# A three-part decoder block on one core: cross attention's scores in 32x128 tiles, low parts in strips, and a few new orders

## The chip, the core and the metric

The kernel runs on one core of one Trainium2 chip. The core has TensorE (PE; its loads of the stationary operand are PEld), VectorE (DVE), ScalarE (ACT), GpSimd (POOL) and the DMA queues that SyncE (SP) issues. The metric is the device time of one execution in microseconds (us), as the median of three. Where times are compared, only what differs by more than a fifth of a per cent is told apart.

## The reference

Everything is fp32, on 32 sequences of 64 tokens with 512 channels. Cut to what matters:

```python
def attn(x, wq, wk, wv, wo):              # 32 heads of 16, 8 key/value heads, causal
    scores = einsum('bihd,bjhd->bhij', q, k) * 16 ** -0.5
    return softmax(where(causal, scores, min)) @ v -> @ wo

def xattn(h, ctx, mask, Wq, Wk, Wv, Wo, q_norm_w, k_norm_w):   # 32 heads of 128, 8 key/value heads
    q = rmsnorm(h @ Wq.T) * q_norm_w
    k = rmsnorm(ctx @ Wk.T) * k_norm_w
    scores = einsum('bhqd,bhkd->bhqk', q, repeat(k, 4)) / sqrt(128) + mask
    return softmax(scores) @ repeat(v, 4) -> @ Wo.T

def ffn(h, ...):                          # shared expert and a latent path
    shared = (relu(h @ up_w) ** 2) @ down_w
    routed = ((h @ fc1_w) @ expert_w) * sum(top_2(h @ gate_w)) @ fc2_w
    return layernorm(shared + routed) * gamma + beta

x = x + attn(layernorm(x)); x = x + xattn(layernorm(x), ctx, mask); x = x + ffn(layernorm(x))
```

## The kernel before

The 32 sequences are worked in two halves of 16 (1024 tokens, 8 tiles of 128 tokens). Each half goes through three stages: self attention, cross attention, and the feed-forward part. The program of each engine is written out by hand as one list of instructions; semaphores (counts) tie the lists together, so the order in which a function calls its helpers is the order on that engine.

The large products are made of three fp32r products each (`split_mm`, L440): high by high, high by low, low by high, where the low part is what the rounding to fp32r left over. ACT makes the high part of a weight piece (`split_piece` of ACT, L938), POOL (L1836) or DVE (L1614) the low one. Weight pieces pass through a ring of three staging buffers (`stage`), and a load waits until the low part of the piece three before it is made.

**Projections of self attention** (`first_projections`, `second_projections`, L598 on for PE): keys/values `kv0` to `kv3`, queries `q0` to `q3`, transposes of normed tiles (`norms`) and of context tiles (`contexts`). `self_attention` (L633) then transposes the keys (`kt0`, `kt1`), makes `q4` and `q5`, and walks 16 sequences: step p makes the scores of sequence p+2, the transposes of the probabilities of p, the value products of p-1, and pieces of output projection. For every sequence DVE spreads the keys over eight groups (L1518), takes maxima and sums, POOL subtracts the maxima (L1866) and multiplies by the reciprocals (L1872), and ACT takes the exponentials. In steps 2, 4, 6 and 8 POOL also makes the low parts of the first four weight pieces of cross attention, two of 512 columns and two of 1024, each with one instruction (L1953).

**Cross attention** runs over 8 groups of heads (one key/value head, four query heads) and 4 chunks of 256 tokens: 32 slots a half, 64 in all. Of a slot, PE's part is `slot` (L791): output projection of chunk k, scores of chunk k+2 (`scores2`, L738), transposes of the probabilities of k+1 (L766), key/value projection of k+4, value product (L782), query projection of k+4. In `scores2` the 128 head channels are cut into four parts of 32 (j), as DVE's transposes leave them; the four 32-token blocks of queries lie in the four row groups of the array (i). The stationary operand of a matmul is 32 channels by 64 columns (two heads of 32 queries), the moving one 32 channels by 64 keys, and the output goes to half of the partitions of bank i of `quad`. So eight tiles of 32x64 of the array are in use in turn. The operands are plain fp32, for which the trace shows two records a matmul.

**Feed-forward** (`last_turn_and_ffn`, PE L805 on): for every chunk of 256 tokens `up` in four parts, `latent`, `down` for two tiles, and `transpose_latent`. The two banks `acc0` and `acc1` take turns in a fixed order (the tables FFN, BETWEEN and LAST), so a matmul group waits until the group two before it has been evacuated. DVE's `result` (L1692) takes the statistics of a finished tile, its normed value (L1706) and adds it to x (L1711, which also needs a value from POOL); `latent_lo` (L1686) evacuates the transposed latent.

Of the kernel before, what the change touches and what calls it, by code (L numbers as in the profile page):

```python
# [7 lines left out]
F32 = mybir.dt.float32  # L8
FR = mybir.dt.float32r
BF16 = mybir.dt.bfloat16  # L10
ALU = mybir.AluOpType
# [6 lines left out]
SEQ = 64  # L18
# [41 lines left out]
SELF_END = "kt0 kt1 q4 q5 q6 q7 lx0 lx1 lx2 lx3 lx4 ckv cq0 cq1"  # L60
# [3 lines left out]
BETWEEN = (FFN + " *ln0 *ln1 latt3 up30 up31 up32 up33 *ln2 *ln3 *ln4 *ln5 *ctx0 *ctx1 *ctx2 *ctx3 *ln6 *ln7 "  # L64
           "*ctx4 *ctx5 *ctx6 *ctx7 " + SELF_END)
# [8 lines left out]
def ffn_numbered(names):  # L74
# [5 lines left out]
        for names in ("kv0 kv1 q0 q1 kv2 q2 kv3 q3", "kv0 kv1 q0 kv2 q1 q2 kv3 q3")]  # L80
# [42 lines left out]
def decoder_block(nc, x_in, ctx_in, mask_in, w_self, w_cross, qn_in, kn_in, w_ffn,  # L123
                  f1g_in, expt_in, fc2_in, gamma_in, beta_in, out):
    with ExitStack() as stack:
# [313 lines left out]
        def _(pe):  # L439
# [177 lines left out]
            def second_projections():  # L617
                self_kv(1, 0)
                norms(1, 4)
                self_kv(1, 1)  # L620
                self_queries(1, 0)
                contexts(1, 0)
                self_kv(1, 2)
                contexts(1, 2)
                self_queries(1, 1)
                norms(1, 6)
                self_queries(1, 2)
                contexts(1, 4)
                self_kv(1, 3)
                contexts(1, 6)  # L630
                self_queries(1, 3)

            def self_attention(half):  # L633
                place = Place(1, half)
                at = place.at
                pe.wait_ge(proj_out.sem, at(proj_out, PROJ[half]["kv3"] + 1))
                for m in range(2):
# [44 lines left out]
                self_queries(half, 4)  # L682
                scores1(0)
# [121 lines left out]
            def last_turn_and_ffn(half):  # L805
# [102 lines left out]
                norm(6)  # L908
                down(0, 1)
                norm(7)  # L910
# [26 lines left out]
        def _(act):  # L937
# [110 lines left out]
            def second_projections():  # L1048
                place = Place(1, 1)
                norms_hi(1, 2)  # L1050
                act.wait_ge(acc_rdy.sem, Place(3, 0).at(acc_rdy, A3[0]["up32"] + 1))
                split_piece(place, 3)
                norms_hi(1, 4)
                self_kv(1, 0)
                self_kv(1, 1)

                act.wait_ge(x_out.sem, Place(3, 0).at(x_out, NT))
                self_queries(1, 0)
                contexts_hi(1, 0)
# [4 lines left out]
                self_queries(1, 1)  # L1064
                norms_hi(1, 6)
                self_queries(1, 2)
                contexts_hi(1, 4)
                split_piece(place, 5)
                self_kv(1, 3)
                contexts_hi(1, 6)  # L1070
                self_queries(1, 3)

            def self_attention(half):
                place = Place(1, half)
                at = place.at
                for m in range(2):
                    n = A1[half][f"kt{m}"]
                    act.wait_ge(acc_rdy.sem, at(acc_rdy, n + 1))
                    nc.scalar.copy(kt[:, m * COLS:(m + 1) * COLS], acc[n % 2][:]).then_inc(acc_free[n % 2].sem, 1)

# [23 lines left out]
                self_queries(half, 4)  # L1104
                def second_norm_hi(i):
                    n_at, n = lx(half, i)
                    transposed_hi(n_at, n, tile_of(xn_hi, i), ln_hi_done)

                for p in range(-AHEAD, NSEQ + 1):
# [23 lines left out]
                    if p in (2, 4, 6, 8):  # L1133

                        if p > 4:
                            act.wait_ge(acc_rdy.sem, at(acc_rdy, A1[half]["q7"] + 1))
                        else:
                            act.wait_ge(proj_rdy.sem, at(proj_rdy, PROJ[half]["kv3"] + 1))
                        split_piece(Place(2, half, 0), (p - 2) // 2)
# [180 lines left out]
        def _(dve):  # L1320
# [147 lines left out]
            def second_projections():  # L1468
                norms_lo(1, 4)
                contexts_lo(1, 0)  # L1470
                first_statistics(1, 6)
                first_statistics(1, 7)
                first_norm(1, 6)
                first_norm(1, 7)
                contexts_lo(1, 2)
                norms_lo(1, 6)
                contexts_lo(1, 4)
                contexts_lo(1, 6)
# [30 lines left out]
            def self_attention(half):  # L1509
                at = Place(1, half).at  # L1510
                def spread_keys(b):

                    if b == 0:
                        evacuated(dve, at, A1[half]["kt0"])
                        evacuated(dve, at, A1[half]["kt1"])
# [106 lines left out]
            def slot(place, k):  # L1622
# [22 lines left out]
            def last_turn_and_ffn(half):  # L1645
# [46 lines left out]
                def result(i):  # L1692
# [11 lines left out]
                    if i >= 2:  # L1704
                        dve.wait_ge(x_out.sem, at(x_out, i - 1))
                    nc.vector.scalar_tensor_tensor(znorm[:, t, :], y[t][:], ymv[:, t, 0:1], gamma,  # L1706
                                                   ALU.subtract, ALU.mult).then_inc(y_free.sem, 1)
                    dve.wait_ge(y_free.sem, at(y_free, i + 1))
# [80 lines left out]
                result(0)  # L1789
                norm_lo(7)  # L1790
                latent_lo(1)
                result(1)
                for q in range(1, CHUNKS):
# [17 lines left out]
                    result(2 * q)  # L1811
# [23 lines left out]
        def _(pool):  # L1835
            def split_piece(place, n):  # L1836
# [5 lines left out]
                                        ).then_inc(w_lo_done, 1)  # L1842

# [81 lines left out]
            def self_attention(half):  # L1925
# [15 lines left out]
                for p in range(-AHEAD, NSEQ):  # L1941
# [10 lines left out]
                    if p in (2, 4, 6, 8):  # L1952
                        split_piece(Place(2, half, 0), (p - 2) // 2)  # L1953
# [159 lines left out]
```

## Time and profile before

| | us |
|---|---|
| median of 3 runs | 1631.0 (1630.46 to 1631.32) |
| the profiled execution | 1630.37 |
| its span (first to last instruction) | 1628.6 |
| PE busy | 1587.8 (97%) |
| PEld busy | 1321.3 (81%) |
| DVE, ACT, POOL busy | 1125.2, 748.0, 630.0 |
| granted TensorE clock | 0.999 of full |

A busy PE is one that has a matmul under way by its modelled end; matmuls overlap, so busy time is not work at the peak rate. What a group of matmuls costs is read from the starts: from the first of it to the first of the next group.

### The profile page before, as it was taken

How to read it: one execution, taken by the hardware profiler on the slowest of the kernel's cores; microseconds unless marked ns; L12 is line 12 of the kernel's file. 1: busy time of each engine (PE TensorE's matmuls, PEld its weight loads, DVE VectorE, ACT ScalarE, POOL GpSimd, SP SyncE). 2: the span in 40 equal slices, each digit the busy share in tenths (PEclk: the TensorE clock that was granted, in tenths of full speed). 3: DMA queues.
4: the chain of work that ended last, by engine and by line, in shares of the span. 5: the costliest groups of instructions: out<-in, count | busy, mean ns of one | idle time of the engine just before them, and what ended most of it. 6: DMA issues, size and time to landing. Idle time of an engine off the chain costs nothing.

```text
span 1628.6 us, 40970 instructions
## 1 busy us (share of the span) xinstructions
PE 1587.8 (97%) x16856; PEld 1321.3 (81%) x16856; DVE 1125.2 (69%) x1983; ACT 748.0 (46%) x1402; POOL 630.0 (39%) x515
## 2 busy tenths in 40 slices
PE   7999999999999999999999899999999999999998
PEld 6667888888888888888886688888888888887887
DVE  6686867667576676885657868667676676668744
ACT  4674544535355354432237745535445444444211
POOL 5683423424243242551228814324243242434401
PEclk9999999999999999999999999999999999999999
DMA  6010202102020120131220002012020120202100
GB/s 228 24 34 1 67 2 64 45 20 64 0 64 25 39 71 0 54 104 46 65 78 27 21 2 67 24 42 64 0 64 19 45 62 2 71 13 57 42 14 27
DMA packets 26285, 71.57 MB, mean 44 GB/s; under 512 B 3168, under 2 KB 3424, under 8 KB 26208
## 3 DMA queue, kind: packets, MB, share of 16 engines
q1 hardware_dynamic: 26208, 70.48, 13.9%
q8 instruction: 56, 0.92, 0.2%
q14 instruction: 21, 0.17, 0.0%
HBM read 66.27 MB, written 4.19 MB: 43 GB/s over the span
## 4 chain that ended last, share of the span: by engine, by line
PE 83%; DVE 8%; POOL 4%; ACT 3%; issue 1%; DMA 0%; SPq 0%; POOLq 0%; DVEq 0%; ACTq 0%
PE acc L441 13%; PE acc L442 13%; PE acc L443 12%; PE y L441 10%; PE y L443 9%; PE y L442 9%; PE quad L753 6%; PE quad L782 4%; PE y L766 2%; POOL prob L1866 1%; DVE psum_ L1530 1%; POOL prob L1872 1%; PE acc L459 1%; POOL w_lo L1841 1%; PE quad L441 1%
## 5 line engine op out<-in xcount | busy, mean ns | idle before, releaser
L1845 POOL TENSOR_TENSOR qkrs<-qkve,mhalf 128x10 f32<-128x10 f32 x64 | 125.0, 1952 | 324.9 <-DVE qkve L1494 324.9
L441 PE MATMUL y<-w_hi 128*128 128x512 f32 x576 | 228.2, 396 | 8.4 <-DVE x L1537 6.0
L443 PE MATMUL y<-w_hi,w_lo 128*128 128x512 f32 x576 | 224.5, 390 | 0.0
L442 PE MATMUL y<-w_lo,w_hi 128*128 128x512 f32 x576 | 224.4, 390 | 0.0
L441 PE MATMUL acc<-w_hi,xn_hi 128*128 128x512 f32 x512 | 207.0, 404 | 0.0
L442 PE MATMUL acc<-w_lo,xn_hi 128*128 128x512 f32 x512 | 201.2, 393 | 0.0
L443 PE MATMUL acc<-w_hi,xn_lo 128*128 128x512 f32 x512 | 199.5, 390 | 0.0
L1841 POOL TENSOR_TENSOR w_lo<-stage,w_hi 128x1024 fp32r<-128x1024 f32 (+1 forms) x88 | 171.0, 1950 | 67.3 <-ACT w_hi L942 63.2
L1399 DVE TENSOR_TENSOR x<-y,x 128x512 f32<-128x512 f32 x128 | 88.3, 690 | 141.7 <-PE y L443 141.7
L1488 DVE TENSOR_REDUCE qkss<-kspace 128x4 f32<-128x512 f32 x128 | 87.3, 682 | 108.9 <-ACT kspace L981 108.2
L441 PE MATMUL acc<-w_hi,cx_hi 128*128 128x256 f32 x512 | 149.7, 292 | 1.7 <-DVE xn_lo L1323 1.7
L1854 POOL TENSOR_TENSOR prob<-prob,pmax 128x512 f32<-128x512 f32 x64 | 69.3, 1082 | 203.0 <-DVE pmax L1382 203.0
L443 PE MATMUL acc<-w_hi,cx_lo 128*128 128x256 f32 x512 | 144.9, 283 | 0.0
L442 PE MATMUL acc<-w_lo,cx_hi 128*128 128x256 f32 x512 | 144.8, 283 | 0.0
L1171 ACT COPY probt<-y 128x512 f32<-128x512 f32 x64 | 37.6, 587 | 232.7 <-PE y L766 232.7
L942 ACT CAST w_hi<-stage 128x1024 fp32r<-128x1024 f32 (+1 forms) x116 | 105.1, 919 | 82.6 <-PE y L443 63.8
L441 PEld LDWEIGHTS y<-w_hi 128*128 128x128 f32 x576 | 108.2, 188 | 33.7 <-issue 11.5
L441 PEld LDWEIGHTS acc<-w_hi,xn_hi 128*128 128x128 f32 x512 | 96.0, 188 | 38.7 <-issue 19.2
L443 PEld LDWEIGHTS y<-w_hi,w_lo 128*128 128x128 f32 x576 | 108.1, 188 | 22.8
L442 PEld LDWEIGHTS y<-w_lo,w_hi 128*128 128x128 f32 x576 | 108.3, 188 | 21.0
L980 ACT COPY qb<-acc 128x512 f32<-128x512 f32 x128 | 75.3, 588 | 101.1 <-PE acc L443 98.3
L1860 POOL TENSOR_TENSOR prob<-prob,prec 128x512 f32<-128x512 f32 x64 | 66.8, 1044 | 137.4 <-DVE prec L1390 137.4
(160 smaller groups left out, 3902.5 us busy)
## 6 DMA issues: line engine op xcount, KB each, us to landing
stage<-in_w_cross SPq DMA_DIRECT2D x64, 512.0 KB, 3.7
stage<-in_w_cross SPq DMA_DIRECT2D x32, 256.0 KB, 2.8
stage<-in_w_ffn SPq DMA_DIRECT2D x16, 512.0 KB, 3.6
stage<-in_w_self SPq DMA_DIRECT2D x8, 512.0 KB, 5.9
out_x<-x SPq DMA_DIRECT2D x16, 256.0 KB, 2.0
x<-in_x SPq DMA_DIRECT2D x6, 512.0 KB, 5.0
kt<-in_ctx SPq DMA_DIRECT2D x8, 256.0 KB, 4.5
prob<-in_ctx SPq DMA_DIRECT2D x8, 256.0 KB, 4.7
```

Source lines behind the costliest of these rows:

```text
L441: nc.tensor.matmul(target, l_hi, r_hi, start=first, stop=False)
L442: nc.tensor.matmul(target, l_hi, r_lo, start=False, stop=False)
L443: return nc.tensor.matmul(target, l_lo, r_hi, start=False, stop=last)
L753: ins = nc.tensor.matmul(quad[h * SEQ:(h + 1) * SEQ, i, t * SEQ:(t + 1) * SEQ], q2t[rows, t, j, 2 * h:2 * h + 2, :].rearrange("p h q -> p ...
L942: nc.scalar.copy(target, stage[:, place.slot(n), 0:width]).then_inc(w_hi_done, 1)
L980: nc.scalar.copy(qraw[:, 2 * (k % 2) + t], blocks(acc[n % 2]))
L1399: nc.vector.tensor_tensor(x[:, i % NT, :], y[i % 2][:], x[:, i % NT, :], ALU.add).then_inc(y_free.sem, 1)
L1488: nc.vector.tensor_reduce(qkss[:, k % 2, t * REP:(t + 1) * REP], qsq[:, t], AX_X, ALU.add).then_inc(q_sum.sem, 1)
L1841: nc.gpsimd.tensor_tensor(low, stage[:, place.slot(n), 0:width], high.bitcast(F32), ALU.subtract).then_inc(w_lo_done, 1)
L1845: return nc.gpsimd.tensor_tensor(target, source, mhalf[:, 0:width], ALU.pow)
L1854: nc.gpsimd.tensor_tensor(pr, pr, spread(pmax[:, buffer, :], 8, SEQ), ALU.subtract).then_inc(s_sub.sem, 1)
L1860: nc.gpsimd.tensor_tensor(pr, pr, spread(prec[:, buffer, :], 8, SEQ), ALU.mult).then_inc(s_nrm.sem, 1)
```

## The change

Six edits go together.

1. `scores2`: one matmul for all four heads (stationary 32x128) where there were two of 32x64; 32 matmuls a slot in place of 64. The output covers all partitions of bank i.
2. Self attention: POOL's low parts of the first four cross-attention pieces in strips of 256 columns, one strip in each of the steps 2 to 13; ACT makes the high parts in steps 1, 3, 5 and 9.
3. The second transposes of keys (`kt1`) after `q4`, on PE, ACT and DVE.
4. Second half, projections: `contexts(1, 4)` and `q2` before `norms(1, 6)`, `q3` before `kv3`; ACT and DVE accordingly.
5. Cross attention on DVE: in the first slot of each group the low part of the output (`outputs_lo`) before `sums`.
6. Feed-forward: tile 7's transposes (`norm(7)`) before `down(0, 1)`; `result` cut in two, with `latent_lo` of the next chunk between its halves for the second tile of a chunk.

```diff
-SELF_END = "kt0 kt1 q4 q5 q6 q7 lx0 lx1 lx2 lx3 lx4 ckv cq0 cq1"
+SELF_END = "kt0 q4 kt1 q5 q6 q7 lx0 lx1 lx2 lx3 lx4 ckv cq0 cq1"
...
-        for names in ("kv0 kv1 q0 q1 kv2 q2 kv3 q3", "kv0 kv1 q0 kv2 q1 q2 kv3 q3")]
+        for names in ("kv0 kv1 q0 q1 kv2 q2 kv3 q3", "kv0 kv1 q0 kv2 q1 q2 q3 kv3")]
@@ PE, second_projections @@
                 self_queries(1, 1)
+                contexts(1, 4)
+                self_queries(1, 2)
                 norms(1, 6)
-                self_queries(1, 2)
-                contexts(1, 4)
+                self_queries(1, 3)
+                contexts(1, 6)
                 self_kv(1, 3)
-                contexts(1, 6)
-                self_queries(1, 3)
@@ PE, self_attention @@
+                transpose_keys(0)
...
                 self_queries(half, 4)
+                transpose_keys(1)
                 scores1(0)
@@ PE, scores2 @@
                         for i in range(4):
                             rows = slice(32 * i, 32 * (i + 1))
                             first = 32 * (1 - i % 2)
-                            for h in range(2):
-                                ins = nc.tensor.matmul(
-                                    quad[h * SEQ:(h + 1) * SEQ, i, t * SEQ:(t + 1) * SEQ],
-                                    q2t[rows, t, j, 2 * h:2 * h + 2, :].rearrange("p h q -> p (h q)"),
-                                    k2t[rows, t, j, first:first + SEQ], start=j == 0, stop=j == 3)
+                            ins = nc.tensor.matmul(
+                                quad[:, i, t * SEQ:(t + 1) * SEQ], q2t[rows, t, j].rearrange("p h q -> p (h q)"),
+                                k2t[rows, t, j, first:first + SEQ], start=j == 0, stop=j == 3)
@@ PE, feed-forward @@
                 norm(6)
+                norm(7)
                 down(0, 1)
-                norm(7)
@@ ACT, self_attention @@
-                    if p in (2, 4, 6, 8):
+                    if p in (1, 3, 5, 9):
@@ DVE, slot @@
+                if k == 0:
+                    outputs_lo(at, k)
                 sums(at, k + 1, (k + 1) % PRING)
-                outputs_lo(at, k)
+                if k > 0:
+                    outputs_lo(at, k)
@@ DVE, feed-forward @@
-                    result(2 * q + 1)
+                    result_norm(2 * q + 1)
                     if q + 1 < CHUNKS:
                         latent_lo(q + 1)
+                    result_added(2 * q + 1)
@@ POOL, self_attention @@
-                    if p in (2, 4, 6, 8):
-                        split_piece(Place(2, half, 0), (p - 2) // 2)
+                    if 2 <= p < 14:
+                        strip = p - 2
+                        if strip < 4:
+                            split_strip(Place(2, half, 0), strip // 2, strip % 2)
+                        else:
+                            split_strip(Place(2, half, 0), 1 + strip // 4, strip % 4)
```

On PE, in a slot of cross attention, the rows around the scores (`quad<-kt,qb`) stood like this before, between the last output projection and the transposes of the probabilities:

```order
L443 MATMUL y<-w_hi,w_lo 128x512
L753 MATMUL quad<-kt,qb 64x64 [waits ot_lo_done,s_add]
L753 MATMUL quad<-kt,qb 64x64 x63
L766 MATMUL y<-ident,prob 128x128 [waits y_free]
L766 MATMUL y<-ident,prob 128x128 x3
```

And now (the shape is that of the output, partitions by columns):

```order
L443 MATMUL y<-w_hi,w_lo 128x512
L754 MATMUL quad<-kt,qb 128x64 [waits ot_lo_done,s_add]
L754 MATMUL quad<-kt,qb 128x64 x31
L766 MATMUL y<-ident,prob 128x128 [waits y_free]
L766 MATMUL y<-ident,prob 128x128 x3
```

The place and the waits are the same; 64 matmuls of half the array's width became 32 of its whole width.

On POOL, steps 6 and 7 of self attention before (`prob` the probabilities, `w_lo` the low part of a weight piece):

```order
L1841 TENSOR_TENSOR w_lo<-stage,w_hi 128x1024 [waits w_hi_done]
L1866 TENSOR_TENSOR prob<-prob,pmax 128x8x32 [waits s_max]
L1845 TENSOR_TENSOR rstd<-veps,mhalf 128x1 [waits ln_veps]
L1872 TENSOR_TENSOR prob<-prob,prec 128x512 [waits s_rec]
L1866 TENSOR_TENSOR prob<-prob,pmax 128x512 [waits s_max]
L1872 TENSOR_TENSOR prob<-prob,prec 128x8x32 [waits s_rec]
L1866 TENSOR_TENSOR prob<-prob,pmax 128x8x32 [waits s_max]
```

And now:

```order
L1867 TENSOR_TENSOR w_lo<-stage,w_hi 128x256 [waits w_hi_done]
L1894 TENSOR_TENSOR prob<-prob,pmax 128x8x32 [waits s_max]
L1873 TENSOR_TENSOR rstd<-veps,mhalf 128x1 [waits ln_veps]
L1900 TENSOR_TENSOR prob<-prob,prec 128x512 [waits s_rec]
L1894 TENSOR_TENSOR prob<-prob,pmax 128x512 [waits s_max]
L1900 TENSOR_TENSOR prob<-prob,prec 128x8x32 [waits s_rec]
L1867 TENSOR_TENSOR w_lo<-stage,w_hi 128x256
L1894 TENSOR_TENSOR prob<-prob,pmax 128x8x32 [waits s_max]
```

The 1024 columns in one instruction after step 6 became 256 columns after each of four steps.

On DVE, the end of a chunk in the feed-forward part before (`ybn` and `qb<-y` are a finished tile's statistics and normed value, `x<-qb` its addition):

```order
L1697 BN_STATS ybn<-y 128x6 [waits y_rdy]
L1706 SCALAR_TENSOR_TENSOR qb<-y,ymv,ksq 128x512 [waits x_out]
L1711 SCALAR_TENSOR_TENSOR x<-qb,yrs,x 128x512 [waits xb_done,y_rs,y_free]
L1323 TENSOR_TENSOR latt_lo<-acc,latt_hi 128x512 [waits latt_hi_done]
L1664 TENSOR_TENSOR qb<-qb 128x512 [waits acc_free1]
```

And now:

```order
L1704 BN_STATS ybn<-y 128x6 [waits y_rdy]
L1713 SCALAR_TENSOR_TENSOR qb<-y,ymv,ksq 128x512 [waits x_out]
L1327 TENSOR_TENSOR latt_lo<-acc,latt_hi 128x512 [waits latt_hi_done]
L1721 SCALAR_TENSOR_TENSOR x<-qb,yrs,x 128x512 [waits xb_done,y_rs,y_free]
L1671 TENSOR_TENSOR qb<-qb 128x512 [waits acc_free1]
```

The evacuation of the transposed latent passed the addition to x (four short rows between the first two are left out in both).

## Rows read from the trace of the kernel before

**Rows 1.** The page: busy time, and the chain that ended last.
```profile
PE 1587.8 (97%) x16856; PEld 1321.3 (81%) x16856; DVE 1125.2 (69%) x1983; ACT 748.0 (46%) x1402; POOL 630.0 (39%) x515
...
PE 83%; DVE 8%; POOL 4%; ACT 3%; issue 1%; DMA 0%; SPq 0%; POOLq 0%; DVEq 0%; ACTq 0%
```

**Rows 2.** Windows, a turn of four slots: length, busy time and count per engine.
```profile
344.00:412.77 68.77, 68.77 (x862) 57.61 (x857) 47.15 (x75) 32.38 (x58) 23.56 (x16) 1.00 0.13 38
```

**Rows 3.** Timeline around one slot's scores: start, length, engine, line, operation.
```profile
412.32 1.46 PEld L753 LDWEIGHTS quad<-kt,qb 32*64 32x64 f32 x128 [0.35 <-issue]
...
413.85 0.42 PEld L766 LDWEIGHTS y<-ident,prob 128*128 128x128 f32 x4
```

**Rows 4.** Windows of L753 alone: length, matmuls under way, loads under way.
```profile
412.34:412.37 0.03, 0.03 (x7) 0.03 (x8) 1.00 0.00 0
412.38:412.42 0.04, 0.04 (x8) 0.04 (x15) 1.00 0.00 0
412.32:412.60 0.28, 0.28 (x32) 0.28 (x33) 1.00 0.00 0
```

**Rows 5.** Groups by form: array tile, operand, count, busy us, mean ns of one.
```profile
L753 PEld LDWEIGHTS quad<-kt,qb 32*64 32x64 f32 x8192 | 93.3, 130 | 22.5 <-issue 21.2 <-DVE qb L1376 1.3
...
L782 PEld LDWEIGHTS quad<-probt,kv 64*128 64x128 f32 x512 | 44.1, 186 | 12.7 <-issue 2.1
L766 PEld LDWEIGHTS y<-ident,prob 128*128 128x128 f32 x256 | 27.0, 140 | 4.8 <-POOL prob L1860 0.6
...
L677 PEld LDWEIGHTS quad<-probt,vbd 128*32 128x32 f32 x512 | 11.7, 108 | 22.4 <-ACT probt L959 17.0 <-issue 5.0
```

**Rows 6.** Windows of L782 (value product, tiles of 64x128) alone, as in Rows 4.
```profile
417.31:417.40 0.09, 0.09 (x2) 0.09 (x2) 1.00 0.00 0
417.42:417.48 0.06, 0.06 (x2) 0.06 (x4) 1.00 0.00 0
```

**Rows 7.** Waits of PE: total us, times, longest us.
```profile
PE acc L441 <- DVE latt_lo L1323: 3.7, 4, 0.9
PE acc L441 <- DVE xn_lo L1323: 3.7, 4, 1.0
...
PE y L441 <- DVE w_lo L1323: 1.9, 2, 1.0
...
PE acc L459 <- DVE cx_lo L1323: 1.4, 1, 1.4
PE acc L441 <- ACT kt L1079: 0.8, 2, 0.4
```

**Rows 8.** Timeline of DVE in self attention: keys spread, every second step from 8 on.
```profile
95.89 1.53 DVE L1518 TENSOR_TENSOR kspace<-kt,gsel 128x512 f32<-128x512 f32 x1
...
107.64 1.52 DVE L1518 TENSOR_TENSOR kspace<-kt,gsel 128x512 f32<-128x512 f32 x1
...
117.55 1.53 DVE L1518 TENSOR_TENSOR kspace<-kt,gsel 128x512 f32<-128x512 f32 x1
```

**Rows 9.** Windows with a 1024-column piece and without: PE, PEld, DVE, ACT, POOL.
```profile
97.00:109.00 12.00, 10.03 (x77) 6.61 (x76) 10.34 (x23) 8.63 (x20) 10.17 (x11) 1.00 0.08 23
109.00:120.00 11.00, 9.85 (x77) 6.88 (x78) 10.78 (x26) 8.19 (x20) 8.21 (x10) 1.00 0.01 2
```

**Rows 10.** Timeline of DVE: first slot of cross attention; end of a feed-forward chunk.
```profile
181.00 0.67 DVE L1387 TENSOR_REDUCE psum_<-prob 128x8 f32<-128x512 f32 x1
...
181.83 1.20 DVE L1323 TENSOR_TENSOR w_lo<-quad,w_hi 128x1024 fp32r<-128x1024 f32 x1
...
764.10 1.71 DVE L1711 SCALAR_TENSOR_TENSOR x<-qb,yrs,x 128x512 f32<-128x512 f32 x1
765.74 0.68 DVE L1323 TENSOR_TENSOR latt_lo<-acc,latt_hi 128x512 fp32r<-128x512 f32 x1
```

**Rows 11.** Timeline of PE in the same place, two matmuls in a row.
```profile
765.15 0.28 PE L442 MATMUL acc<-xn_lo,w_hi 128*128 128x256 f32 x1
765.27 0.28 PE L443 MATMUL acc<-xn_hi,w_lo 128*128 128x256 f32 x1
```

More of the change, by code:

```diff
@@ L59 @@
        "up10 up11 up12 up13 lat20 lat21 latt2 up20 up21 up22 up23 lat30 lat31")
-SELF_END = "kt0 kt1 q4 q5 q6 q7 lx0 lx1 lx2 lx3 lx4 ckv cq0 cq1"
+SELF_END = "kt0 q4 kt1 q5 q6 q7 lx0 lx1 lx2 lx3 lx4 ckv cq0 cq1"
 FIRST = ("*ln0 *ln1 *ln2 *ln3 *ln4 *ln5 *ctx0 *ctx1 *ln6 *ln7 "
          "*ctx2 *ctx3 *ctx4 *ctx5 *ctx6 *ctx7 " + SELF_END)
-BETWEEN = (FFN + " *ln0 *ln1 latt3 up30 up31 up32 up33 *ln2 *ln3 *ln4 *ln5 *ctx0 *ctx1 *ctx2 *ctx3 *ln6 *ln7 "
-           "*ctx4 *ctx5 *ctx6 *ctx7 " + SELF_END)
+BETWEEN = (FFN + " *ln0 *ln1 latt3 up30 up31 up32 up33 *ln2 *ln3 *ln4 *ln5 *ctx0 *ctx1 *ctx2 *ctx3 *ctx4 *ctx5 "
+           "*ln6 *ln7 *ctx6 *ctx7 " + SELF_END)
 LAST = FFN + " latt3 up30 up31 up32 up33"
@@ L635, in self_attention, with transpose_keys @@
                 at = place.at
-                pe.wait_ge(proj_out.sem, at(proj_out, PROJ[half]["kv3"] + 1))
-                for m in range(2):
+                def transpose_keys(m):
+                    pe.wait_ge(proj_out.sem, at(proj_out, PROJ[half][f"kv{2 * m + 1}"] + 1))
                     to = acc_bank(at, A1[half][f"kt{m}"])
@@ L1064, in second_projections @@
                 self_queries(1, 1)
+                contexts_hi(1, 4)
+                self_queries(1, 2)
                 norms_hi(1, 6)
-                self_queries(1, 2)
-                contexts_hi(1, 4)
                 split_piece(place, 5)
+                self_queries(1, 3)
+                contexts_hi(1, 6)
                 self_kv(1, 3)
-                contexts_hi(1, 6)
-                self_queries(1, 3)
             def self_attention(half):
@@ L1075, in self_attention, with keys_out @@
                 at = place.at
-                for m in range(2):
+                def keys_out(m):
                     n = A1[half][f"kt{m}"]
@@ L1079, in self_attention @@
                     nc.scalar.copy(kt[:, m * COLS:(m + 1) * COLS], acc[n % 2][:]).then_inc(acc_free[n % 2].sem, 1)
+                keys_out(0)
                 def spread_values(b):
@@ L1104, in self_attention @@
                 self_queries(half, 4)
+                keys_out(1)
                 def second_norm_hi(i):
@@ L1132, in self_attention @@
                         spread_values(p + 2)
-                    if p in (2, 4, 6, 8):
-                        if p > 4:
+                    if p in (1, 3, 5, 9):
+                        n = (1, 3, 5, 9).index(p)
+                        if n > 1:
                             act.wait_ge(acc_rdy.sem, at(acc_rdy, A1[half]["q7"] + 1))
                         else:
-                            act.wait_ge(proj_rdy.sem, at(proj_rdy, PROJ[half]["kv3"] + 1))
-                        split_piece(Place(2, half, 0), (p - 2) // 2)
+                            act.wait_ge(proj_rdy.sem, at(proj_rdy, 8))
+                        split_piece(Place(2, half, 0), n)
                 first = Place(2, half, 0)
@@ L1475, in second_projections @@
                 contexts_lo(1, 2)
+                contexts_lo(1, 4)
                 norms_lo(1, 6)
-                contexts_lo(1, 4)
                 contexts_lo(1, 6)
@@ L1511, in spread_keys @@
                 def spread_keys(b):
-                    if b == 0:
-                        evacuated(dve, at, A1[half]["kt0"])
-                        evacuated(dve, at, A1[half]["kt1"])
+                    if b % (NSEQ // 2) == 0:
+                        evacuated(dve, at, A1[half][f"kt{2 * b // NSEQ}"])
                     if b >= 2:
@@ L1690, in latent_lo, with result_norm @@
                          latt_hi[:].rearrange("p l t -> p (l t)")).then_inc(acc_free[n % 2].sem, 1)
-                def result(i):
+                def result_norm(i):
                     t = i % 2
@@ L1707, in result, with result_added @@
                                                    ALU.subtract, ALU.mult).then_inc(y_free.sem, 1)
+                def result_added(i):
+                    t = i % 2
                     dve.wait_ge(y_free.sem, at(y_free, i + 1))
@@ L1788, in last_turn_and_ffn @@
                 norm_lo(6)
-                result(0)
                 norm_lo(7)
+                result_norm(0)
+                result_added(0)
                 latent_lo(1)
-                result(1)
+                result_norm(1)
+                result_added(1)
                 for q in range(1, CHUNKS):
@@ L1810, in last_turn_and_ffn @@
                         first_norm(1, i + 1)
-                    result(2 * q)
+                    result_norm(2 * q)
+                    result_added(2 * q)
                     if q >= 2 and half == 0:
@@ L1842, in split_piece, with split_strip @@
                                         ).then_inc(w_lo_done, 1)
+            def split_strip(place, n, strip):
+                if strip == 0:
+                    pool.wait_ge(w_hi_done, place.piece(n)[1] + 1)
+                high, width = piece_target(place.stage, n, 0)
+                low, _ = piece_target(place.stage, n, 1)
+                c = slice(strip * 256, (strip + 1) * 256)
+                ins = nc.gpsimd.tensor_tensor(low[:, c], stage[:, place.slot(n), c], high[:, c].bitcast(F32),
+                                              ALU.subtract)
+                if (strip + 1) * 256 == width:
+                    ins.then_inc(w_lo_done, 1)
             def rsqrt(target, source, width):
```

1 line of the change is left out of this document (removed).

## The prediction

> **What bounds the kernel now.** Look first at the shares of busy time and at the chain that ended last. PE is busy in 97% of the span, and 83% of the chain runs over it; DVE has 8%, POOL 4%, ACT 3% [rows 1]. Then at one turn of cross attention: in 68.77 us PE is never idle, DVE is busy for 47 us, POOL for 24 [rows 2]. So in the 64 slots an edit counts by what it does to PE's own work, and the other engines have room. All waits of PE are listed in one view, and they are few; the reader is to see there which of them the new orders touch [rows 7]. They lie outside the steady turns: in the projections, in self attention, in the first slot and in the feed-forward part.
>
> **Edit 1, the scores.** The stage runs from its first load at 412.32 to the first load of the next stage at 413.85: 1.53 us. Its loads span 1.46 of these, and 0.07 follow [rows 3]. It has 128 pairs of a load and a matmul for 64 matmuls in the program, over eight tiles of the array, so 16 pairs a tile. After the change there are 64 pairs over four tiles: again 16 pairs a tile. A tile streams the same 64 key columns in each pair. So the array's streaming work isn't less; only the number of instructions is halved, while each load carries 128 columns instead of 64.
>
> What does a load of 128 columns cost? The mean length goes by columns and not by rows: 108 ns for 32 columns of 128 rows, 130 for 64 columns of 32 rows, 186 for 128 columns of 64 rows [rows 5]. More telling is when the next load into the same tile may start. In the scores now, eight loads are under way until 412.37, and by 412.42 seven of the second round have joined: 0.054 us after the first round [rows 4]. In the value product, whose two tiles are 64x128, two loads are under way until 417.40 and four from 417.42: the second load of a tile starts some 0.11 us after the first [rows 6]. Twice the columns, twice the time. The two tiles load side by side, so row groups don't disturb each other, and I take the same for four.
>
> The Trainium skill ("TensorE: Matmul & The Clock Gate", section on LDWEIGHTS) has this as a rule that speaks against the change: a load takes its columns over 1.2 GHz, and one of 32x128 as long as one of 128x128. By it a round would be 107 ns; the trace agrees for 64x128 with its 0.11, and it has no load of 32x128.
>
> A pair streams for about 0.05 us, so with loads of 0.11 the loads set the pace in each tile. The new stage: 15 rounds of 0.11, 0.02 for the four tiles' offset, 0.19 for the last load, and the 0.07 behind it, 1.93 us. That is 0.40 more than 1.53, and 64 times 0.40 is **25.6 us more**. Nothing hides it, since PE has no idle time in these slots [rows 2]. From above: if no load overlapped the one before it in its tile, a round would take the whole 0.186, and the stage 3.1; the value product excludes it, as its second load starts while the first runs [rows 6]. With 0.12 a round it is 2.08, 35 us in all. From below: if the loads cost nothing and a round were today's 0.054, 15 x 0.054 + 0.05 + 0.13 + 0.07 = 1.06, about 1.1 with a hand-over or two, 27 us less in all. There is one row near that end: the loads of the transposes, also 128 columns, last 140 ns and not 186 [rows 5]; but these are in the transposes' own form, and the value product is plain fp32 as the scores are. I take its 0.11.
>
> **Edits 3 and 4, projections.** In the second half PE waits 1.4 us for a context tile's low part, with the normed tiles 6 and 7 queued in front of other work; now q2, twelve matmuls of 512 columns, comes first, and I count the wait as gone. The wait for the copy of the keys, 0.8 in two places, is covered by q4, which now stands between the two transposes [rows 7]. A wait is counted from the modelled end of the matmul before, which lies some 0.16 us behind the place where the next could have started (one lasts 0.28 and the next starts 0.12 after it [rows 11]); three places add 0.5. Together **2.7 less**.
>
> **Edit 5.** At the first slot of each half PE waits 0.95 for `w_lo` of the output (1.9 in two) [rows 7]. On DVE the sums stand ahead of it: 181.00 to 181.83 [rows 10]. Passing them gives 0.83, twice: **1.7 less**. What is moved back is the sums, on which POOL and the next transposes wait; in steady slots DVE has over 5 us to spare a slot [rows 2], so I count no cost.
>
> **Edit 6, feed-forward.** PE waits 3.7 us in four places for `latt_lo` and, of the waits for `xn_lo`, 1.0 in each half where tile 7's transposes came after `down(0, 1)` [rows 7]. `latt_lo` stands on DVE behind an addition of 1.71 us, 764.10 to 765.74 [rows 10]. Without it the evacuation comes 1.64 earlier than PE's wait of 0.92 needs. Tile 7 has the whole of `down(0, 1)` for its evacuation. So 3.7 + 2.0 and six times 0.16: **6.7 less**. The addition is done 0.6 later, which delays a store that nobody waits for.
>
> **Edit 2, strips.** Two steps with a 1024-column piece take 11.75 us (95.89 to 107.64), two without 9.91 [rows 8]: 1.84 for each such piece, of which there are four in the program, 7.4 in all. The pieces of 512 may give something too. But the strips don't vanish. They put about 0.6 us of POOL (a quarter of a piece) into each of steps 10 to 13, where DVE is busy for 10.78 of 11.00 us and POOL for only 8.21 [rows 9]; so part is given back. Bounds: 7.4 and 2 more from the small pieces at best, 5 lost at worst (four steps of 0.6, twice) without any gain; I take **6 less**, nearer to the rows with and without a piece.
>
> **Sum.** 25.6 - 2.7 - 1.7 - 6.7 - 6 = 8.5 more. The profiled execution took 1630.4 (span 1628.6 and 1.8 around it), so 1638.9; the median of the runs is 0.6 above the profiled one, so **1639.5 us**.
>
> **Rivals.**
>
> *Issue sets the pace, and halving the instructions pays.* For it: the first 32 matmul records of the stage start within 0.28 us [rows 4]; the other 96 need about 1.53 - 0.28 - 0.07 = 1.18, 12.3 ns each, while the tiles could take one every 0.054/8 = 6.7 ns. So today the stage is held by something else than its loads and streams, which is probably how fast PE is fed. With 64 records that limit is 0.28 + 32 x 0.0123 = 0.67, and if wide loads were as quick as narrow ones, the stage would fall to about 1.1: 27 less, and with the 17 of the other edits 44 less, **1587 us**. Against it: Rows 6. It decides as soon as a round is under 0.087 us, since 15 x 0.087 + 0.02 + 0.13 + 0.07 is today's 1.53. The skill has a rule on this side too (the same page, on the gap from matmul to matmul): small matmuls follow each other no closer than about 25 ns. By it 32 fewer would be worth 0.8 us a slot; this trace, with 1.53/64 = 24 ns for each matmul in the program, agrees with the size.
>
> *The wide loads cost as much as the saved instructions give.* A stage of about 1.5, so only the 17 of the other edits: **1614 us**. It needs a round of 0.087, for which no row speaks.
>
> *Strips that hurt.* Steps 10 to 13 get 0.6 longer each in both halves, 5 us, and the shorter steps 6 to 9 give only that back: the 6 of edit 2 fall away, **1645.5 us**. For it: DVE's 98% in these steps [rows 9]. Against: POOL had 2.8 us free there.
>
> **Chances and range.** Forecast 65%, strips that hurt 12%, issue 15%, even 8%. The forecast's own range: loads from 23 (0.107 a round) to 31, the other edits from 10 to 21: 1633 to 1652. The whole range leaves out the issue case and the ends, and reaches to the even case: **1612 to 1651**. A difference of 0.2% (3.3 us) is about what this measurement tells from none. Slower by more than that: nearly all of the first two cases, 73%. Within it: 5%, where small losses meet large gains. Faster: 22%.
>
> **What would show it.** Right, if the scores' stage is 1.9 us, its loads are 186 ns long on average and the second round starts 0.11 after the first, and if a steady slot grows from 17.19 (68.77/4) to 17.6. Wrong, if the stage is 1.5 or less: then the 17 us decide alone. For the other edits: no wait for `latt_lo`, none for the context's low part or the keys' copy, `w_lo` under 0.2 a place, and step pairs in self attention of about 10 us from 6 to 13. If those are still 11 or more, edit 2 failed.

## The result, and the profile after

The changed kernel takes 1639.81 us (median of 5, 1638.89 to 1641.31) against 1631.32 of the kernel before in the same series (1630.46 to 1632.85): a ratio of 1.0051, 95% interval 1.0036 to 1.0066. That is 8.5 us slower. The profiled execution has a span of 1637.2 us, 8.6 more than before.

The page's first rows. PE has 4096 matmul records fewer (2048 matmuls of the program, at two records each) and as many loads, and is busy 23 us longer:

```profile
PE 1611.1 (98%) x12760; PEld 1348.2 (82%) x12760; DVE 1116.9 (68%) x1983; ACT 748.8 (46%) x1402; POOL 635.0 (39%) x531
...
PE 88%; DVE 6%; POOL 2%; ACT 2%; issue 1%; DMA 0%; POOLq 0%; DVEq 0%; ACTq 0%
```

A turn of four slots of cross attention (windows; columns as in [rows 2]):

```profile
341.22:411.66 70.44, 70.44 (x594) 59.28 (x593) 46.71 (x74) 32.49 (x58) 23.54 (x17) 1.00 0.12 37
```

So a slot is 17.61 us where it was 17.19, with PE without a gap in both. The timeline of PE's loads around one slot's scores answers to [rows 3]:

```profile
413.03 1.88 PEld L754 LDWEIGHTS quad<-kt,qb 32*128 32x128 f32 x64 [0.35 <-issue]
414.97 0.31 PEld L766 LDWEIGHTS y<-ident,prob 128*128 128x128 f32 x3
```

The stage is 1.94 us from its first load to the next stage's (1.53 before). The group by form answers to [rows 5], and the windows on the line of the scores (matmuls, then loads under way) to [rows 4] and [rows 6]:

```profile
L754 PEld LDWEIGHTS quad<-kt,qb 32*128 32x128 f32 x4096 | 120.1, 186 | 22.4 <-issue 21.1 <-DVE qb L1380 1.3
```
```profile
413.06:413.12 0.06, 0.06 (x4) 0.06 (x4) 1.00 0.00 0
413.17:413.20 0.03, 0.03 (x6) 0.03 (x8) 1.00 0.00 0
```

A load lasts 186 ns, as in the value product, not 130 as before. Four loads are under way until 413.12, and only by 413.17 have the next four joined.

The waits of PE, which answer to [rows 7]:

```profile
PE acc L459 <- DVE xn L1347: 7.2, 2, 6.3
PE y L441 <- DVE x L1540: 2.5, 8, 0.5
PE quad L679 <- DVE w_lo L1327: 2.1, 6, 0.5
PE acc L441 <- DVE xn_lo L1327: 1.7, 2, 0.9
...
PE acc L459 <- DVE cx_lo L1327: 1.4, 1, 1.4
```

`latt_lo` and `w_lo` ahead of an output projection are gone, 2.0 of `xn_lo` too, and the copy of the keys. But 1.4 us for the context's low part is still there, which the prediction had counted as gone. In self attention DVE's spreading of the keys in steps 8, 10 and 12 answers to [rows 8]:

```profile
93.21 1.53 DVE L1521 TENSOR_TENSOR kspace<-kt,gsel 128x512 f32<-128x512 f32 x1
...
103.13 1.52 DVE L1521 TENSOR_TENSOR kspace<-kt,gsel 128x512 f32<-128x512 f32 x1
...
113.05 1.53 DVE L1521 TENSOR_TENSOR kspace<-kt,gsel 128x512 f32<-128x512 f32 x1
```

Both step pairs take 9.92 us, where they took 11.75 and 9.91. The strips in the later steps cost nothing, though each holds POOL for 0.73 to 1.23 us and not for the 0.6 that the prediction gave it.

Where the time went, read from when the same matmul starts in both traces (after minus before, the difference that each stretch adds):

| stretch | us |
|---|---|
| start to the first value product, first half | -0.8 |
| self attention, 3.7 in each half | -7.3 |
| 64 stages of scores, 0.418 each | +26.7 |
| first slot of cross attention, beside its own 0.418, 1.2 in each half | -2.3 |
| feed-forward, three places of 1.2 in each half (tile 7's transposes, two chunk ends) | -7.3 |
| projections of the second half | -0.5 |
| sum | 8.5 (the spans differ by 8.5 before rounding) |

Only part of the first row belongs to the change: the second key transposes give 0.45 there. The rest lies ahead of them, where two traces of the same program can be 1.6 us apart (orders_ctx_first and orders_filled, below).

### The profile page after: what moved, and what is told of

It reads as the page before. It is cut to its first block, busy times and chain, and to the rows that moved or that the text cites. A ratio compares the mean times of both kernels' runs of the same rounds, so it can differ in the third digit from the quotient of the medians.

```text
span 1637.2 us, 32796 instructions
## 1 busy us (share of the span) xinstructions
PE 1611.1 (98%) x12760; PEld 1348.2 (82%) x12760; DVE 1116.9 (68%) x1983; ACT 748.8 (46%) x1402; POOL 635.0 (39%) x531
## 4 chain that ended last, share of the span: by engine, by line
PE 88%; DVE 6%; POOL 2%; ACT 2%; issue 1%; DMA 0%; POOLq 0%; DVEq 0%; ACTq 0%
PE acc L441 14%; PE acc L442 13%; PE acc L443 13%; PE y L441 10%; PE y L442 9%; PE y L443 9%; PE quad L754 8%; PE quad L782 4%; PE y L766 2%; DVE psum_ L1533 1%; PE acc L459 1%; POOL prob L1894 1%; POOL prob L1900 1%; PE quad L441 1%; DVE pmax L1528 1%
## 5 line engine op out<-in xcount | busy, mean ns | idle before, releaser
L1856 POOL TENSOR_TENSOR w_lo<-stage,w_hi 128x1024 fp32r<-128x1024 f32 (+1 forms) x80 | 156.3, 1962 | 62.0 <-ACT w_hi L942 57.9
L754 PEld LDWEIGHTS quad<-kt,qb 32*128 32x128 f32 x4096 | 120.1, 186 | 22.4 <-issue 21.1
L754 PE MATMUL quad<-kt,qb 32*128 32x64 f32 x4096 | 128.8, 273 | 0.5 <-issue 0.5
```

Of the source, the lines that this page charges most:

```text
L754: ins = nc.tensor.matmul(quad[:, i, t * SEQ:(t + 1) * SEQ], q2t[rows, t, j].rearrange("p h q -> p (h q)"), k2t[rows, t, j, first:first + S ...
L1856: nc.gpsimd.tensor_tensor(low, stage[:, place.slot(n), 0:width], high.bitcast(F32), ALU.subtract).then_inc(w_lo_done, 1)
```

## Experiments

My theory: in a tile the load of 128 columns takes 0.11 us and the next can't start before it is through, so that 16 rounds of loads make the stage, whatever the matmuls stream. The rivals for the slower stage: the wide matmuls' streams set it; four tiles in the row groups have a round of 0.11 however wide the load. For the other edits: that they only worked with or against the wider stage. Edits 3, 5 and 6 were not taken back one by one; their shares are read from their places in the traces.

### The parts by themselves

**scores_only.** The kernel before with this edit alone:

```diff
-                            for h in range(2):
-                                ins = nc.tensor.matmul(
-                                    quad[h * SEQ:(h + 1) * SEQ, i, t * SEQ:(t + 1) * SEQ],
-                                    q2t[rows, t, j, 2 * h:2 * h + 2, :].rearrange("p h q -> p (h q)"),
+                            ins = nc.tensor.matmul(
+                                quad[:, i, t * SEQ:(t + 1) * SEQ], q2t[rows, t, j].rearrange("p h q -> p (h q)"),
```

> The kernel before with the 32x128 scores alone. If the scores' stage costs 0.42 us more in each of 64 slots and nothing hides it, 26.9 us more than before: ratio 1.0165, a steady slot of 17.61 us. Rival: some of the cost exists only together with the new orders (a wait that they cover or uncover); then the difference to before is off 26.9 by more than 3 us.

1658.16 us against 1632.83 of before: ratio 1.0155, interval 1.0141 to 1.0169, so 25.3 us more; the slot is 17.61 by the distance of its stages. Its stage in the timeline:

```profile
418.38 1.88 PEld L752 LDWEIGHTS quad<-kt,qb 32*128 32x128 f32 x64 [0.35 <-issue]
420.33 0.31 PEld L764 LDWEIGHTS y<-ident,prob 128*128 128x128 f32 x3
```

It is the same 1.94 as in the changed kernel. The cost stands by itself.

**orders_only.** The changed kernel with the edit above taken back.

> The changed kernel with the scores in tiles of 32x64 again. If the parts add up: 26.9 us less than the changed kernel, 18.4 less than before, about 1612.5, ratio 0.9885, slot 17.19. Rival: the wider stage had bought slack for DVE that the orders need; then less than 15 is left.

1613.96 us: ratio 0.9886 (0.9871 to 0.9901), 18.9 less than before, with the stage at its old length:

```profile
409.46 1.45 PEld L755 LDWEIGHTS quad<-kt,qb 32*64 32x64 f32 x128 [0.35 <-issue]
410.98 0.42 PEld L768 LDWEIGHTS y<-ident,prob 128*128 128x128 f32 x4
```

The parts add up within what the runs can tell: 25.3 - 18.9 = 6.4, and the whole gave 8.5; each of these has 2 to 3 us of uncertainty.

**orders_no_strips.** On top of orders_only:

```diff
-                    if 2 <= p < 14:
-                        ...
+                    if p in (2, 4, 6, 8):
+                        split_piece(Place(2, half, 0), (p - 2) // 2)
@@ ACT @@
-                    if p in (1, 3, 5, 9):
+                    if p in (2, 4, 6, 8):
```

> As orders_only, but POOL makes the low parts of the first four cross-attention pieces whole again, in steps 2, 4, 6 and 8. If the 3.7 us that each self attention lost in the changed kernel come from the strips, this is 7.4 us slower than orders_only (about 1620), with waits of 1.1 us for x back in the steps 7 to 10. Rival: they come from the split key transposes and other orders around; then the same as orders_only within 2 us.

1621.96 us, ratio 0.9938 (0.9924 to 0.9952): 8.0 slower than orders_only. The waits of PE from 50 to 135 us, of this kernel:

```profile
PE y L441 <- DVE x L1542: 3.0, 5, 1.1
PE quad L679 <- ACT probt L961: 1.3, 2, 0.7
PE quad L679 <- ACT vbd L1095: 0.7, 2, 0.4
```

And of orders_only:

```profile
PE y L441 <- DVE x L1542: 1.3, 4, 0.5
PE quad L679 <- DVE w_lo L1329: 0.9, 2, 0.5
```

From its first value product to its last, self attention shifts against the kernel before by 0.0 in each half of this kernel, and by -3.6 and -3.7 in orders_only. So the new places of POOL's low parts and ACT's high parts, which were taken back together, give 7.3, and neither the key transposes nor anything else around them has a part in it. That it is the pieces of 1024 columns is seen on DVE: its spreading of the keys gains 1.8 us over each of the two pieces in a half, and next to nothing before them.

**orders_ctx_first.** On top of orders_only, on DVE:

```diff
                 first_statistics(1, 7)
+                contexts_lo(1, 2)
                 first_norm(1, 6)
                 first_norm(1, 7)
-                contexts_lo(1, 2)
```

> As orders_only, but on DVE, in the second half's projections, the low parts of context tiles 2 and 3 go before the norms of tiles 6 and 7. My theory of the wait that edit 4 did not take away: PE waits for the bank that DVE still has to empty for context tile 3, and DVE is held by a norm of 2.6 us in front of it, whatever PE transposes next. Then the wait of 1.4 us for cx_lo goes: 1.4 to 1.6 us faster than orders_only, in one place. Rival: the wait only changes its name, to the norm of tile 6 or 7, as POOL's w_lo piece runs beside it; then no gain.

1613.91 us, ratio 0.9879 (0.9864 to 0.9894): by the medians not to be told from orders_only. The traces tell more, since they can be compared place by place. In the changed kernel DVE stood like this (timeline):

```profile
839.03 0.55 DVE L1347 TENSOR_SCALAR xn<-x,mv,rstd 128x512 f32<-128x512 f32 x1
840.01 2.61 DVE L1347 TENSOR_SCALAR xn<-x,mv,rstd 128x512 f32<-128x512 f32 x1 [0.44 <-POOL rstd L1873]
842.54 1.28 DVE L1327 TENSOR_TENSOR cx_lo<-acc,cx_hi 128x512 fp32r<-128x512 f32 x2
```

And here:

```profile
829.40 1.29 DVE L1329 TENSOR_TENSOR cx_lo<-acc,cx_hi 128x512 fp32r<-128x512 f32 x2 [0.38 <-ACT cx_hi L948]
830.61 2.15 DVE L1349 TENSOR_SCALAR xn<-x,mv,rstd 128x512 f32<-128x512 f32 x2
```

PE has no wait at all between 825 and 850 us, and the shift against orders_only goes from +0.74 before this place to -1.01 behind it: 1.75 us, a little over the 1.4 to 1.6 expected. The theory of the wait holds; its worth is under what the runs can tell.

### What sets the pace of the scores

The first four of these were each run once and compute other scores than the kernel needs, or only half of them; they are read by their slot. **wide_move96** is the changed kernel with more moving columns:

```diff
-                                quad[:, i, t * SEQ:(t + 1) * SEQ], ...
-                                k2t[rows, t, j, first:first + SEQ], start=j == 0, stop=j == 3)
+                                quad[:, i, t * SEQ:t * SEQ + 96], ...
+                                k2t[rows, t, j, 0:96], start=j == 0, stop=j == 3)
```

> The changed kernel, with 96 moving columns in each matmul of the scores in place of 64 (so the scores hold other values). Theory, loads of 128 columns set the pace at 0.11 us a round: 96 columns stream in 0.08, still below it, so the stage stays at 1.95 us and a steady slot at 17.61, or 0.03 more for the last matmul. Rival, the streams of the wide tiles set it: half as long again a round, 0.16, and the slot 0.8 longer, 18.4.

```profile
415.35 1.88 PEld L754 LDWEIGHTS quad<-kt,qb 32*128 32x128 f32 x64 [0.35 <-issue]
417.32 0.31 PEld L766 LDWEIGHTS y<-ident,prob 128*128 128x128 f32 x3
```

1642.51 us, slot 17.64: the 0.03 more is the last matmul's. **wide_move32** has `t * SEQ:t * SEQ + 32` and `first:first + 32` in the same places.

> The changed kernel with 32 moving columns in each matmul of the scores, so half of the scores is not computed. Theory (loads): slot stays at 17.6 (17.58 to 17.61). Rival (streams of the wide tiles): round 0.055, slot 0.87 shorter, 16.7.

```profile
412.92 1.88 PEld L754 LDWEIGHTS quad<-kt,qb 32*128 32x128 f32 x64 [0.35 <-issue]
414.84 0.42 PEld L766 LDWEIGHTS y<-ident,prob 128*128 128x128 f32 x4
```

1639.02 us, slot 17.59. Over a factor of three in what is streamed, the loads' span stays at 1.88. The streams of the wide tiles don't set the pace.

**narrow_half** is orders_only with `for h in range(1)`.

> As orders_only, but only the first two of the four heads: 32 matmuls of 32x64 on four tiles, so as many instructions as in the changed kernel and the same moving columns, each load half as wide; half of the scores is not computed. Theory: rounds of 0.054 to 0.058 as no feeding limit binds at 32 matmuls... if it binds it is 12.3 ns a record over 64 records, 0.8 at most: stage 1.0 to 1.2, slot 16.7 to 16.85. Rival: four tiles in row groups always take 0.11 a round, however wide the load: slot 17.6.

```profile
403.39 1.02 PEld L755 LDWEIGHTS quad<-kt,qb 32*64 32x64 f32 x64 [0.35 <-issue]
404.48 0.42 PEld L768 LDWEIGHTS y<-ident,prob 128*128 128x128 f32 x4
```

1591.51 us, slot 16.75, stage 1.09. This has as many loads and matmuls as the changed kernel, on as many tiles, with the same moving columns; only the load is 64 columns wide and not 128, and the loads' span is 1.02 and not 1.88. That is the cleanest pair: the width of the load is the cost. By the starts of the loads in the two traces, the rounds of the narrow tiles settle at 0.058 us and those of the wide ones at 0.112.

It also shows that two narrow loads of one row group go side by side. The first 0.22 us of the stage (windows of the scores' line; matmuls, then loads under way), in the kernel before with eight tiles:

```profile
412.32:412.54 0.22, 0.22 (x24) 0.22 (x32) 1.00 0.00 0
```

And in narrow_half with four:

```profile
403.39:403.61 0.22, 0.22 (x12) 0.22 (x16) 1.00 0.00 0
```

Four rounds in the same time, with 8 loads a round or with 4. Only after the 32nd load does the kernel before fall behind this pace.

**narrow_move32** is orders_only with half of the moving columns.

> As orders_only with 32 moving columns in each of the 64 matmuls; half of the scores is not computed. It tells what holds the stage of before at 1.53 us. If the feeding of PE with instructions: 1.5 still, slot 17.17 to 17.19. If streams and loads of the eight tiles by turns: a round gets 0.03 to 0.05 shorter, slot 16.4 to 16.8.

```profile
407.33 1.37 PEld L755 LDWEIGHTS quad<-kt,qb 32*64 32x64 f32 x128 [0.35 <-issue]
408.74 0.42 PEld L768 LDWEIGHTS y<-ident,prob 128*128 128x128 f32 x4
```

1607.93 us, slot 17.07, stage 1.41. It meets neither of my two cases and lies much nearer to the first: half the streaming gives 0.11 of 1.52. In narrow_half half the instructions, on half of the tiles, give 0.43. Since eight tiles kept the pace of four for the first 32 loads, the likely reading is that the stage of before is held mostly by the number of its instructions. What in their feeding holds it is not shown.

**narrow_h_outer** is orders_ctx_first with the loops over i and h exchanged:

```diff
-                        for i in range(4):
-                            ...
-                            for h in range(2):
+                        for h in range(2):
+                            for i in range(4):
```

> As orders_ctx_first, with the two column halves outermost of a group of eight matmuls of the scores (four row groups, then again), where the two halves of a row group followed each other. If PE's feeding sets the stage of 1.52 us, the order of the tiles doesn't matter: slot 17.19, the same time. Rival: the halves of a row group hinder each other's loads: slot up to 0.4 shorter, 25 us less.

1613.01 us, ratio 0.9890 (0.9874 to 0.9907), slot 17.19. The loads' span:

```profile
409.64 1.46 PEld L755 LDWEIGHTS quad<-kt,qb 32*64 32x64 f32 x128 [0.35 <-issue]
```

The order of the tiles doesn't matter, so the stage of before isn't held by the two loads of a row group standing next to each other.

### A version that beats both

**orders_filled.** On top of orders_ctx_first, on PE behind self attention:

```diff
                 project_chunk_q(first, 0)
+                for h in (0, 1):
+                    project_part(at, NT - 1, NT, h, y[1], NT - 2)
                 second_norm(5)
                 second_norm(6)
+                for h in (2, 3):
+                    project_part(at, NT - 1, NT, h, y[1], NT - 2)
                 project_chunk_kv(first, 1)
                 project_chunk_q(first, 1)
-                project_out(at, NT - 1, NT)
```

> As orders_ctx_first, but the last output projection of self attention (tile 7), which stood behind the query projection of chunk 1, is cut in two halves of six matmuls, one ahead of the transposes of normed tiles 5 and 6 and one behind them. There PE waited 0.83 and 0.87 us; the twelve matmuls fill both, 1.0 each with the hidden part, in two halves of the kernel: 4 us less than orders_ctx_first, about 1610, ratio 0.9865. Second part: the clock row that falls to half of full for 3.4 us behind these waits in some executions (1.5 us lost) should not be seen there again. Rival: the later wait is for DVE's chain (sums of squares, normed tile, scaling) and only moves to the scores of chunk 0; then less than 1 us.

1608.02 us against 1631.26, ratio 0.9862 (0.9845 to 0.9878): 23.2 less than before. That is 5.9 less than orders_ctx_first, which was measured in another series; each against the kernel before of its own series, it is 4.3. Its waits of PE from 125 to 165 us:

```profile
PE acc L441 <- ACT ksq L977: 0.4, 1, 0.4
...
PE acc L459 <- ACT kspace L986: 0.2, 1, 0.2
```

Of 0.83 and 0.87 there remain 0.2 and 0.4; by the starts in the traces each half gains 0.8 there and 0.4 more up to its first slot, so I had asked too much of it with 2. The first half gains another 1.5 from the clock, told at the end. The rest of the difference to orders_ctx_first lies before the first key transposes (1.6, in a stretch that no edit touches) and in the range of the runs. narrow_h_outer, which is as fast as orders_ctx_first and was measured in the same series as this version, takes 1613.01, 5.0 more, and its fastest run is slower than the slowest here. So the version is faster; of the difference the traces give 2.4 us to the filled places.

## Why the prediction was right

1639.5 was forecast, 1639.8 measured. The terms, beside what the traces gave:

| step | forecast | found |
|---|---|---|
| edit 1: 0.40 a stage | +25.6 | +26.7 (0.418); alone 25.3 by the runs |
| edit 2: strips | -6 | -7.3 |
| edits 3 and 4: projections | -2.7 | -1.1, all of it edit 3 |
| edit 5: first slot | -1.7 | -1.6 in orders_only, -2.3 with the wider stage |
| edit 6: feed-forward | -6.7 | -7.3 |
| start, ahead of any edit | 0 | -0.3 |
| sum | 8.5 | 8.5 by the medians, 8.4 by these rows |

**Edit 1** held in its mechanism. The decisive step was to ask of each load not how long it lasts on average but when the next one into the same tile may begin, in a form of the same width with other rows. The value product had given 0.11, the changed kernel has 0.112. The 0.02 missing in the stage is 15 rounds of 0.0017, and it is the 1.1 us by which edit 1 was put too low. The rule of the Trainium skill ("TensorE: Matmul & The Clock Gate", section on LDWEIGHTS), that a 32x128 load takes as long as a 128x128 one, is borne out: 186 ns with 32 rows here, 188 for the 128x128 loads of the output projection. The page's formula gives 107 ns for 128 columns, an estimate; it lies near the 112 from load to load in a tile, not at the length of a record. Nor do the columns alone fix that length: the transposes' loads of 128x128 last 140 ns in both kernels.

**The rival of issue** was half right, and this is why it had to be priced. The number of instructions probably did hold most of the stage of before (narrow_move32, narrow_half), and halving it with loads as cheap as the narrow ones would have given 0.43 a slot, as in narrow_half. It fell since halving it by doubling the width raises the other limit, 16 rounds of a tile, from 0.9 (0.058 each) to 1.8 (0.112 each).

**Strips.** The part that I gave back was not lost: the steps 10 to 13 did not get longer (9.92 where 9.91 before), although DVE had been busy for 98% of them and the strips took POOL more than 0.6 us. The price per piece, 1.84, stands in the trace as 11.75 - 9.92 = 1.83 for each piece, with four of them 7.3. The way it is lost can be read in the kernel before (timeline of POOL, then of ACT):

```profile
102.95 2.39 POOL L1841 TENSOR_TENSOR w_lo<-stage,w_hi 128x1024 fp32r<-128x1024 f32 x1 [1.08 <-ACT w_hi L942]
105.31 0.61 POOL L1866 TENSOR_TENSOR prob<-prob,pmax 128x256 f32<-128x256 f32 x1
```
```profile
105.95 0.42 ACT L955 ACTIVATE prob<-prob 128x256 f32<-128x256 f32 x1 [1.79 <-POOL prob L1866]
```

The subtraction of the maximum queues on POOL behind the piece, and ACT's exponential waits for it. In the changed kernel the same wait is 0.8.

**Edit 4 failed at one step.** I wrote that "now q2 ... comes first, and I count the wait as gone". In the new order q2 does not come first: `contexts(1, 4)` stands ahead of it, as the list of the change says. The wait's label, `cx_lo`, said that the wait is for a bank that holds a context tile and not for a normed tile. Whatever transposes PE does next need the bank of context tile 2 (the expectation of orders_ctx_first names tile 3), and the new order only put context tile 4 in the place of a normed tile. PE's timeline in the changed kernel:

```profile
843.37 1.23 PE L459 MATMUL acc<-ident,kt 128*128 128x128 f32 x8 [1.42 <-DVE cx_lo L1327]
```

On DVE the low part for tile 2 starts at 842.54, behind a norm of 2.6 us, where the norm before it takes 0.55; the longer one runs beside a piece of POOL's (see the last section). orders_ctx_first, which moves the low part ahead of the norms, takes the wait away. By the starts in the traces edit 4 changed nothing, and edit 3 gave the 1.1 that was counted for it.

So five terms were off, and they nearly cancel. Edit 1 cost 1.1 more than forecast and the projections gave 1.6 less; against that, strips, edit 5 and feed-forward gave 1.3, 0.6 and 0.6 more. The mechanism of each but edit 4 is as worked out; that the total came within 0.3 us is partly luck.

**Edits 5 and 6** went as worked out: `w_lo` starts right behind the scaling, and the evacuation of the latent runs before the addition (waits gone in the list above). That the first slot gives 1.2 in each half of the changed kernel and not 0.8 is because the wider stage ahead of it gives DVE time: in scores_only, without edit 5, 0.4 of that stage's cost is already covered there in each half (the waits for `w_lo` fall from 1.9 to 1.1 in two places).

## What to carry to other kernels

Merging small matmuls pays by the number of instructions and costs by the width of the load. Before doing it, work out how long one tile takes from load to load, and compare the sum of its rounds with the time that the stage takes now. In this case (32 channels, plain fp32, 32 to 96 moving columns) the tile of 128 columns took 0.112 us a round whatever it streamed, and the tile of 64 took 0.058, two of them side by side in a row group; so the wider tiles lost. Other forms were not measured. And a wait belongs to the bank or tile in its label; reordering the engine that waits helps only if what comes first doesn't need the same one.

## What the runs showed of the hardware

Three things stand out. The loads' span of 1.88 us for 64 loads didn't change by 0.01 between 32, 64 and 96 moving columns: up to 96 columns, what streams in a tile is wholly hidden under its loads of 128 columns, but for the last matmul's 0.03 us for 32 columns.

The second is that some of DVE's instructions take several times as long beside a low part on POOL. In the changed kernel DVE's norm (`xn<-x,mv,rstd`, 128x512) takes 0.54 us with nothing under way on POOL, and its scaling of the queries (`qb<-qb,qkrs`, 128x1024) 1.21. Five of these norms take 2.6 us and 16 of these scalings 3.4; all 21 start 0.06 to 0.11 us after a low part of 1024 columns on POOL and end after it. One of them is the norm in front of the context's low part, beside this row of POOL's timeline:

```profile
839.95 2.38 POOL L1856 TENSOR_TENSOR w_lo<-stage,w_hi 128x1024 fp32r<-128x1024 f32 x1
```

Another is the scaling at 177.65 in the kernel before (3.42 us), ahead of the output's low part that edit 5 moves. What holds DVE there no run tells: none takes the piece on POOL away from beside it and leaves the rest.

The third is the clock, and this I had not expected. Windows of orders_only, around the two waits behind self attention and just behind them (seventh number: the granted share of the clock):

```profile
142.00:145.80 3.80, 2.10 (x15) 1.52 (x14) 2.02 (x4) 2.15 (x4) 1.08 (x1) 1.00 0.00 0
145.90:149.20 3.30, 3.30 (x18) 3.30 (x17) 2.45 (x5) 0.00 (x0) 0.78 (x1) 0.50 0.02 5
```

PE was busy for 2.10 of 3.80 us, and then it ran at 0.50 of full, 1.2 GHz, and did 18 matmuls. The same stretch in the changed kernel, where it was busy for 2.20 and kept the whole clock:

```profile
142.00:145.80 3.80, 2.20 (x17) 1.99 (x18) 2.19 (x5) 1.65 (x4) 1.96 (x1) 1.00 0.02 4
145.90:149.20 3.30, 3.30 (x22) 2.96 (x21) 3.27 (x7) 0.87 (x2) 0.00 (x0) 1.00 0.00 0
```

And in orders_filled, which has work in the place of the waits:

```profile
142.00:145.80 3.80, 3.80 (x27) 3.38 (x26) 2.39 (x5) 1.55 (x3) 1.96 (x1) 1.00 0.02 4
```

The dip lasts 3.4 us and costs 1.5 where it comes: from the last value product to the first scores orders_only loses 1.5 against the kernel before, orders_no_strips nothing. It was there in the traces of orders_only, orders_ctx_first, narrow_h_outer, wide_move96, narrow_half and narrow_move32, in the second half's same place in scores_only, wide_move32 and again narrow_half, and not in those of before, after, orders_no_strips and orders_filled. So one execution of a kernel has it and, I think, another has not: with it orders_only's profiled execution took 1614.7 us, and another of its runs, of which only the time and a mean clock of 1.0 are known, 1612.7. It also bears on scores_only: its profiled span is 27.7 us above that of before, with the dip, and its median 25.3. That filling the waits prevents it was seen in one trace alone, and stays a likely reading.
